# The six-layer stage: own tables of places for each engine and batch, hand-over by single banks, norm steps on VectorE and ScalarE

## The chip, the cores and the metric

The kernel runs on one core of one Trainium2 chip. Its time is the device time of one execution in microseconds; the kernel before takes 3076.7 us (median of 3 runs, 3075.34 to 3079.2). Another execution was recorded by the hardware profiler, and the rows below are from that one.

The engines are PE (TensorE), DVE (VectorE), ACT (ScalarE), POOL (GpSimd) and SP (SyncE, which only issues transfers here). Each executes its own list of instructions in order. They meet only at semaphores: an instruction with an unmet wait holds back everything behind it on its engine. All matrix products land in PSUM, which has 8 banks of 2 KB in each of 128 partitions; one bank holds a 128x512 product in f32.

## The reference

The program is four residual blocks on x of shape (2, 512, 128): a cross-attention transformer block (stage A), an attention block with 31 routed experts (stage B), six layers of self-attention, cross-attention and feed-forward (stage C), and a block with 64 experts (stage D). The change is in stage C only. What it computes, per batch of two:

```
for i in range(6):                                   # D=128, 16 heads of 8, DFF=512, context 77
    xn = adaln(x, noise, n1_w[i], n1_b[i])           # layernorm, then scale and shift
    q, k, v = split(xn @ qkv_w[i].T)
    x = x + attn(rope(q), rope(k), v, src_mask) @ so_w[i].T       # 512 x 512 scores, 16 heads
    xn = adaln(x, noise, n2_w[i], n2_b[i])
    x = x + attn(rope(xn @ cq_w[i].T), rope(ctx @ ck_w[i].T),
                 ctx @ cv_w[i].T, ctx_mask) @ co_w[i].T           # 512 x 77 scores
    xn = adaln(x, noise, n3_w[i], n3_b[i])
    x = x + gelu(xn @ f1_w[i].T + f1_b[i]) @ f2_w[i].T + f2_b[i]
```

## The kernel before

Stage C (`stage_c`, line 1372) works through 12 units: unit n is layer n // 2 of batch n % 2. A unit starts from the result of unit n - 2, so that two chains of six units run beside each other.

A unit is: layernorm statistics on DVE (`stats`), the reciprocal root, the normalised tiles, four transposes on PE (`turn_norm`) and the scale and shift on ACT (`copy_norm`, into `hT`). Then the products for q, k (each with a rotated twin) and v. Since the scores are computed from bf16 operands without loss, q and k are cut into three bf16 parts on DVE, ACT and POOL, and 12 transfers on SP stack these parts in `qs` and `ks` (`stack`).

Self-attention takes 32 tiles twice. In the first pass `scores` multiplies and DVE takes the row maxima (`row_max`, L2042); each tile is two products, one for each half of the array's rows (`hp` 0 is partitions 0 to 63, `hp` 1 is 64 to 127), in PSUM banks 0 and 1. The maxima of a quarter are split in two bf16 parts, turned on PE (`turn_max`), copied by ACT and stacked as two more rows of `qs` by SP (`stack_max`). In the second pass `scores_T` multiplies again, transposed, with the maximum already subtracted (banks 2 and 3), ACT takes the exponential (`exps`, L1899), and PE weighs the values (`weigh`, L1525, bank 4). The sums go by ACT (`copy_sums`), PE (`turn_back`) and DVE (`normalise`) into `cn`.

Cross-attention has the same two passes in smaller form (`cross_max` with L2097 on DVE, `cross_T` with L1943 on ACT, `weigh_x`, `turn_back_x`). Everything but the two large passes shares a ring of three banks (5, 6, 7) through `fill`, `arrived` and `drained`: a bank's next use waits for the last one's reader.

In the kernel before, the norm is shared by two engines. DVE takes the statistics and a bit-trick seed of the reciprocal root (`seed_steps`); POOL then does three Newton steps of four small operations (`newton_steps`, L102 to L105) and writes the four normalised tiles (`apply`, L1831).

What sets the order of the work: each engine's list is written out by the same double loop over windows of 48 places, and the same tables serve all engines and both batches. `S_AT`, `ST_AT` and `W_AT` say at which place the tiles of the two passes stand, the `C_...` names where the other steps stand. Unit n's first pass begins in window n; its second pass runs into the next one; its cross-attention and feed-forward (`rest`) are in window n + 1, beside the self-attention of unit n + 1; the start of unit n + 2 (`begin`) comes at places 32 to 41 of that window. At one place an engine takes the steps in a fixed sequence: score products, `rest`, `begin`, `weigh` and the turns. `scores(n, i)` and `scores_T(n, j)` emit both halves in a row.

## Time and profile before

| | us |
|---|---|
| median of 3 runs | 3076.7 |
| the profiled execution | 3073.5 |
| its span | 3071.7 |
| stage C in it, from its first statistics of a unit (1082.67) to its last addition of a unit (begins 2818.84) | 1736.2 |
| its steady part, 1118 to 2694 | 1576, of which PE busy 1271.7 |
| two units (2027.96 to 2301.03) | 273.07 |

Most of the rows are of three kinds. A window row gives the busy time of every engine in a stretch and the granted clock of TensorE, where 1.00 is 2.4 GHz and 0.50 is 1.2 GHz. A timeline row is one instruction or a run of equal ones: its start, its length, and in square brackets how long the engine had been idle before it and what ended that. A row of groups gives the number of instructions, their busy time in all and the mean of one. PE's busy time counts each product up to its modelled end, so two products that run side by side, or one behind the other in the pipeline, overlap in it.

### The profile page before, as it was taken

Reading aid. Unit: us, or ns where it says so; the run is one execution under the profiler, and the core shown is the slowest. Engines: PE = TensorE matmul, PEld = TensorE weight load, DVE = VectorE, ACT = ScalarE, POOL = GpSimd, SP = SyncE. Lnnn points to the kernel's source line nnn. Section 1 sums busy time; section 2 is a strip of 40 time slices with the busy share of each in tenths; the row PEclk is TensorE's granted clock in tenths of the full one; section 3 lists DMA queues with packets and bytes.
Section 4 is the critical chain, followed back from the end, with each engine's and each line's share of the span. In section 5 each row is a group of like instructions: output and inputs, shape, how many; then the busy total and the mean of one; then the engine's idle time right before and its main releaser. Section 6 shows DMA issues by size and latency. Waiting matters only on the chain. (4 is left out here: it accounts for less than half of the span.)

```text
span 3071.7 us, 31900 instructions
## 1 busy us (share of the span) xinstructions
PE 2470.8 (80%) x11288; PEld 978.6 (32%) x11288; DVE 1591.5 (52%) x3349; ACT 1113.9 (36%) x1840; POOL 344.5 (11%) x719
## 2 busy tenths in 40 slices
...
GB/s 123 1 1 1 0 1 1 97 1 1 1 1 1 10 72 21 1 21 1 36 1 21 36 1 21 1 36 1 21 19 18 21 1 21 1 1 85 1 0 7
DMA packets 38095, 54.33 MB, mean 18 GB/s; under 512 B 5137, under 2 KB 34610, under 8 KB 36402
## 3 DMA queue, kind: packets, MB, share of 16 engines
...
## 5 line engine op out<-in xcount | busy, mean ns | idle before, releaser
L2042 DVE TENSOR_REDUCE C_nm<-ps 128x1 f32<-128x512 f32 x768 | 491.3, 684 | 384.3 <-PE ps L1489 375.2
L1899 ACT ACTIVATE C_prob<-ps 128x512 f32<-128x512 f32 x768 | 415.3, 593 | 324.0 <-PE ps L1510 300.3
L1489 PE MATMUL ps<-C_ks,C_qs 62*128 62x512 bf16 x768 | 253.2, 496 | 102.3 <-DVE C_nm L2042 82.8
L1510 PE MATMUL ps<-C_qs,C_ks 64*128 64x512 bf16 x768 | 214.8, 446 | 51.3 <-ACT C_prob L1899 41.5
L1525 PE MATMUL ps<-C_prob,C_va 128*32 128x512 f32 x1536 | 233.7, 688 | 0.4
L1489 PEld LDWEIGHTS ps<-C_ks,C_qs 62*128 62x128 bf16 x768 | 50.9, 97 | 365.8 <-DVE C_nm L2042 233.9
L102 POOL TENSOR_TENSOR lnt<-rs 128x4 f32<-128x4 f32 x108 | 21.4, 198 | 1278.6 <-DVEq L2036 1272.9
L1606 PE MATMUL ps<-C_kc,C_qx 32*128 32x308 f32 x384 | 122.1, 724 | 29.3 <-DVE C_nmx L2097 13.0
L1943 ACT ACTIVATE C_u<-ps,C_biasx 77x512 f32<-77x512 f32 x192 | 120.7, 677 | 68.2 <-PE ps L1633 61.2
L1629 PE MATMUL ps<-C_qx,C_kc 32*77 32x512 f32 x384 | 128.7, 749 | 20.4 <-ACT C_u L1943 11.6
L714 DVE TENSOR_REDUCE A_nm<-ps 128x2 f32<-128x1024 f32 x64 | 77.5, 1212 | 113.8 <-PE ps L497 113.6
L1564 PE MATMUL ps<-ident,xn 128*128 128x128 f32 x144 | 35.6, 394 | 121.1 <-POOL xn L1831 121.1
L2064 DVE RECIPROCAL C_rden<-ps 128x16 f32<-128x16 f32 x96 | 24.6, 256 | 198.3 <-PE ps L1533 134.8
L1921 ACT ACTIVATE C_hT<-ps,aff 128x512 f32<-128x512 f32 x36 | 28.0, 777 | 267.4 <-PE ps L1564 267.4
L1831 POOL TENSOR_SCALAR xn<-y,mv,rs 128x128 f32<-128x128 f32 x144 | 112.4, 793 | 3.9
L2097 DVE TENSOR_REDUCE C_nmx<-ps 128x4 f32<-128x308 f32 x192 | 82.8, 473 | 51.0 <-PE ps L1610 50.5
L1571 PE MATMUL ps<-C_hT,C_w 128*128 128x512 f32 x144 | 101.8, 847 | 5.5 <-ACT C_hT L1921 5.5
L647 ACT ACTIVATE A_p<-ps 128x1024 f32<-128x1024 f32 x64 | 65.6, 1025 | 112.1 <-PE ps L525 112.1
L647 ACT ACTIVATE B_p<-ps 128x1024 f32<-128x1024 f32 (+1 forms) x64 | 45.0, 703 | 146.6 <-PE ps L529 146.6
L1510 PEld LDWEIGHTS ps<-C_qs,C_ks 64*128 64x128 bf16 x768 | 48.5, 98 | 150.5 <-ACT C_prob L1899 104.0
L455 PE MATMUL ps<-hT,B_w 128*128 128x512 f32 x128 | 75.6, 674 | 23.4 <-DVE B_rot L709 12.2
L1303 DVE SCALAR_TENSOR_TENSOR y<-ps,B_gates,y 128x128 f32<-128x128 f32 x256 | 71.9, 344 | 42.0 <-PE ps L1257 42.0
...
## 6 DMA issues: line engine op xcount, KB each, us to landing
...
B_w<-in_B_ew SPq DMA_DIRECT2D x8, 514.0 KB, 10.5
...
```

Of the source, the lines that this page charges most:

```text
L647: act.activation(prob[:, n % 2, kt, :, q0:S], ps[:, ST_BANK:ST_BANK + 2, q0:S], ACT.Exp, scale=SCALE)\
L1489: pe.matmul(ps[:, S_BANK + hp, :], lhsT=qs[side(hp, MAX_ROW), b, 2 * q + pq, t * P:(t + 1) * P], rhs=ks[side(hp, MAX_ROW), b, 2 * q + pq, ...
L1510: pe.matmul(ps[:, ST_BANK + hp, :], lhsT=ks[side(hp, HALF), b, 2 * q + pq, kt * P:(kt + 1) * P], rhs=qs[side(hp, HALF), b, 2 * q + pq, :], ...
L1525: last = pe.matmul(ps[ct * VW:(ct + 1) * VW, PV_BANK, :], lhsT=va[:, b, kt, q * QUAD + ct, :], rhs=prob[:, kt % 2, ct // 2, ct % 2, :], st ...
L1571: pe.matmul(ps[:, bank, :], lhsT=weight(n, col), rhs=hT[:], start=True, stop=True)\
L1606: pe.matmul(ps[:, banks[gh], 0:4 * CTX], lhsT=qx[rows, t * P:(t + 1) * P], rhs=cross.k[rows, c, :, :], start=True, stop=False)
L1629: pe.matmul(ps[0:CTX, banks[gh], :], lhsT=cross.k[rows, c, j, :], rhs=qx[rows, :], start=True, stop=False)
L1831: ins = pool.tensor_scalar(m.xn[:, k, :], m.y[:, k, :], m.mv[:, t, 0:1], m.rs[:, t:t + 1], ALU.subtract, ALU.mult)
L1899: act.activation(prob[:, kt % 2, pq, hp, :], ps[:, ST_BANK + hp, :], ACT.Exp, scale=SCALE)\
L1943: act.activation(probx[:, q % 2, jj, gh, :], ps[0:CTX, bank, :], ACT.Exp, bias=cross.bias[:, b:b + 1], scale=SCALE).then_inc(emptied[bank], 1)
L2042: dve.tensor_reduce(nm[:, q % 2, t, pq, hp:hp + 1], ps[:, S_BANK + hp, :], AX.X, ALU.max, negate=True).then_inc(max_done, 1)
L2097: dve.tensor_reduce(nmx[:, t, 8 * gp + 4 * gh:8 * gp + 4 * gh + 4], ps[:, bank, 0:4 * CTX].rearrange("p (j k) -> p j k", k=CTX), AX.X, ALU ...
```

## The change

Four things change, all in stage C.

1. Each engine gets its own table for even units (batch 0) and odd units (batch 1): `TENSOR`, `VECTOR`, `SCALAR`, `GPSIMD`, `SYNC`. A table gives each step a place; `WINDOW` is 1128, unit n's places are counted from 1128 n, and an engine's list is all its steps sorted by that sum (`timeline`). Places of a unit reach from 208 to 2456 (even) and from 0 to 2242 (odd).
2. The two halves of a score tile, the twins of q, k and the cross query, and the four products and four gelus of the feed-forward become steps with places of their own. A wait for the previous reader then covers one bank rather than a pair. The semaphore of the parts is divided in one for q and one for k, and k comes before q.
3. The norm: all of the reciprocal root is now on DVE (`rstd_steps`, 12 small operations, and one for minus mean times root), and the product and shift that make the normalised tiles are four `Identity` activations on ACT (`apply`). POOL keeps one addition and two subtractions for k, the copy of `vx` and the bias.
4. The rotated cross query uses `hT` of the norm's buffer (`m.hT`) instead of a part of `rot`; `copy_norm` waits for the last reader of `hT`. The zeroing of `qs` and `ks` on POOL no longer stands behind a norm.

```diff
-WINDOW = 48
-S_AT = [1, 2, 2, 3, 4, 5, 5, 6, 7, 8, 9, 11, 12, 13, 14, 15,
+WINDOW = 1128
+TENSOR = (
+    {"S": [453, 464, 469, 485, 501, 518, 534, 551, 567, 584, 598, 615, 620, 636, 641, 658, 670, 675, 694, 702,
...
+def timeline(tables):
+    return sorted({(n * WINDOW + s, n, s) for n in range(UNITS) for slots in tables[n % B].values() for s in slots})
...
-        rotx = rot[:, 0, :, :]
+        rotx = m.hT
...
-                def scores(n, i):
+                def scores(n, i, hp):
...
-                    for hp in range(2):
-                        if n or i:
-                            pe.wait_ge(max_done, 2 * (n * TILES + i) + hp - 1)
-                        pe.matmul(ps[:, S_BANK + hp, :],
...
+                    if n or i:
+                        pe.wait_ge(max_done, 2 * (n * TILES + i) + hp - 1)
+                    pe.matmul(ps[:, S_BANK + hp, :],
...
-                cp = Chain(pool, order_p)
-
-                def apply(n, count):
-                    pool.wait_ge(seeded, count)
-                    newton_steps(cp, pool, m, TB)
-                    for t in range(TB):
-                        k = n % B * TB + t
-                        ins = pool.tensor_scalar(m.xn[:, k, :], m.y[:, k, :], m.mv[:, t, 0:1], m.rs[:, t:t + 1],
-                                                 ALU.subtract, ALU.mult)
...
+                def apply(n, count):
+                    act.wait_ge(seeded, count)
+                    for t in range(TB):
+                        k = n % B * TB + t
+                        ins = act.activation(m.xn[:, k, :], m.y[:, k, :], ACT.Identity, bias=m.lnu[:, t:t + 1],
+                                             scale=m.rs[:, t:t + 1])
+                    ins.then_inc(xn_ready, 1)
...
-                    seed_steps(c_, dve, m, TB, False)
-                    dve.sem_inc(seeded, 1)
+                    rstd_steps(c_, dve, m, TB, False)
+                    dve.scalar_tensor_tensor(m.lnu[:, 0:TB], m.mv[:, 0:TB, 0], -1.0, m.rs[:, 0:TB], ALU.mult, ALU.mult)\
+                        .then_inc(seeded, 1)
...
-                    for i in ((0, 1, 2), (3,))[k]:
-                        bank = fill(("ff", c, i))
-                        pe.matmul(ps[:, bank, :], lhsT=weight(c, LF1 + i * P), rhs=hT[:], start=True, stop=True)\
-                            .then_inc(filled[bank], 1)
+                    bank = fill(("ff", c, i))
+                    pe.matmul(ps[:, bank, :], lhsT=weight(c, LF1 + i * P), rhs=hT[:], start=True, stop=True)\
+                        .then_inc(filled[bank], 1)
...
-                for n in range(UNITS + 1):
-                    for s in range(WINDOW):
-                        if n:
-                            score(n - 1, s + WINDOW)
...
+                for _, n, s in timeline(TENSOR):
+                    step(n, s)
```

Some places of the tables, odd units: on PE the products of the first pass stand at 235 to 1047 and those of the second at 456 to 1350, the first cross score step at 1569, the feed-forward's last step at 2206. On DVE the maxima stand 8 places apart where they are densest, the three norms' statistics at 0, 1453 and 2046. Even units: first pass 453 to 1328, second 755 to 1526, first cross score step 1749, last step 2419 on PE and 2456 on DVE.

Three pieces of the lists follow, each before and after. PE, at the first pass over the cross scores of a batch, beside the other batch's self-attention. `C_kc,C_qx` and `C_krowc,C_onesc` are one half of a cross score step (keys and mask row), `C_ks,C_qs` a product of the first pass, `C_qs,C_ks` one of the second. Before:

```order
L1606 MATMUL ps<-C_kc,C_qx 128x308 x2
L1610 MATMUL ps<-C_krowc,C_onesc 128x308 x2
L1489 MATMUL ps<-C_ks,C_qs 128x512 x2
L1510 MATMUL ps<-C_qs,C_ks 128x512 x2
L1618 MATMUL ps<-identb,C_nmpx 128x128 x4
L1629 MATMUL ps<-C_qx,C_kc 77x512 x2
```

and after:

```order
L1675 MATMUL ps<-C_ks,C_qs 128x512
L1791 MATMUL ps<-C_kc,C_qx 128x308 x2
L1795 MATMUL ps<-C_krowc,C_onesc 128x308 x2
L1675 MATMUL ps<-C_ks,C_qs 128x512 x2
L1803 MATMUL ps<-identb,C_nmpx 128x128 x4
L1675 MATMUL ps<-C_ks,C_qs 128x512
L1814 MATMUL ps<-C_qx,C_kc 77x512 x2
L1818 MATMUL ps<-C_nmTx,C_selx 77x512 x2
```

Where a round held one cross step, a pair of the first pass and a pair of the second, it now holds one cross step and one or two single products of the first pass.

DVE, from the addition of an attention's result (`y<-y,ps`) over the statistics to the seed of the norm. Before:

```order
L2042 TENSOR_REDUCE C_nm<-ps 128x1 x8
L2072 TENSOR_TENSOR y<-y,ps 128x512
L2028 BN_STATS st<-y 128x6 x4
L2031 BN_AGGR mv<-st 128x2 x4
L93 TENSOR_SCALAR lnv<-mv 128x4
L94 TENSOR_SCALAR lnt<-lnv 128x4
L95 TENSOR_SCALAR rs<-lnt 128x4
L2042 TENSOR_REDUCE C_nm<-ps 128x1 x8
```

and after:

```order
L2205 TENSOR_TENSOR y<-y,ps 128x512
L2175 TENSOR_REDUCE C_nm<-ps 128x1
L2161 BN_STATS st<-y 128x6 x4
L2164 BN_AGGR mv<-st 128x2 x4
L2175 TENSOR_REDUCE C_nm<-ps 128x1
L93 TENSOR_SCALAR lnv<-mv 128x4
L94 TENSOR_SCALAR lnt<-lnv 128x4
L95 TENSOR_SCALAR rs<-lnt 128x4
L79 TENSOR_TENSOR lnt<-rs 128x4
L80 SCALAR_TENSOR_TENSOR lnu<-lnt,lnv 128x4
L81 SCALAR_TENSOR_TENSOR rs<-lnu,rs 128x4
```

The last three rows come three times, and one `lnu<-mv,rs` (L2169) behind them; single maxima stand between the parts of the norm.

ACT, around the third norm and the feed-forward of an odd unit (`C_prob` is an exponential of the second pass, `C_cT` the copy of the turned context, `xn` the normalised tiles, `C_hT` the scale and shift, `C_u` with x4 the gelus). Before:

```order
L1899 ACTIVATE C_prob<-ps 128x512 x6
L1915 ACTIVATE C_cT<-ps 128x512
L1910 ACTIVATE C_nmT<-ps 8x512
L1899 ACTIVATE C_prob<-ps 128x512 x2
L1921 ACTIVATE C_hT<-ps,aff 128x512
L1899 ACTIVATE C_prob<-ps 128x512 x2
L1956 ACT_TABLE_LOAD
L1956 ACTIVATE C_u<-ps,C_w 128x512 x4
```

and after:

```order
L2034 ACTIVATE C_prob<-ps 128x512 x7
L2039 ACTIVATE C_cw<-ps 128x512
L2034 ACTIVATE C_prob<-ps 128x512
L2065 ACTIVATE xn<-y,lnu,rs 128x128 x4
L2034 ACTIVATE C_prob<-ps 128x512 x2
L2058 ACTIVATE C_hT<-ps,aff 128x512
L2034 ACTIVATE C_prob<-ps 128x512 x2
L2138 ACT_TABLE_LOAD
L2138 ACTIVATE C_u<-ps,C_w 128x512 x4
```

The four tiles of the norm have come in, two exponentials ahead of the scale and shift; the gelus stay together between two table loads.

## Rows read from the trace of the kernel before

**Rows 1.** The page: busy time of each engine, share of the span, instructions.

```profile
PE 2470.8 (80%) x11288; PEld 978.6 (32%) x11288; DVE 1591.5 (52%) x3349; ACT 1113.9 (36%) x1840; POOL 344.5 (11%) x719
```

**Rows 2.** Windows: stretch, its length, busy time of each engine, PEclk granted clock.

```profile
1118.00:2694.00 1576.00, 1271.70 (x6083) 442.56 (x6081) 791.24 (x1790) 727.51 (x1284) 242.83 (x585) 0.77 0.05 15
2028.00:2301.10 273.10, 220.62 (x1066) 77.34 (x1066) 134.23 (x305) 127.08 (x224) 43.80 (x106) 0.78 0.06 16
2048.50:2055.30 6.80, 2.40 (x4) 0.40 (x4) 4.67 (x13) 0.00 (x0) 4.74 (x16) 0.50 0.00 0
2069.00:2089.00 20.00, 17.60 (x70) 5.29 (x70) 12.23 (x26) 6.20 (x11) 0.00 (x0) 0.50 0.00 1
2089.40:2123.60 34.20, 30.70 (x208) 10.22 (x204) 16.71 (x36) 25.14 (x45) 0.00 (x0) 1.00 0.01 1
```

**Rows 3.** Waits of PE from 1118 to 2694: total us, times, longest.

```profile
PE ps L1489 <- DVE C_nm L2042: 82.8, 113, 3.0
PE ps L1564 <- POOL xn L1831: 78.1, 33, 3.2
PE ps L1510 <- ACT C_prob L1899: 38.1, 70, 0.8
```

**Rows 4.** Timeline: a unit's stage C start, end, and same step two units apart.

```profile
1082.67 0.87 DVE L2028 BATCH_NORM_STATS2 st<-y 128x6 f32<-128x128 f32 x4
1117.70 0.61 PE L1489 MATMUL ps<-C_ks,C_qs 62*128 62x512 bf16 x2 [16.14 <-DMA C_ks<-C_parts]
2027.96 0.58 SPq L1761 DMA_DIRECT2D C_qs<-C_parts  x1
2301.03 0.58 SPq L1761 DMA_DIRECT2D C_qs<-C_parts  x1
2818.84 0.69 DVE L2122 TENSOR_TENSOR y<-y,ps 128x512 f32<-128x512 f32 x1 [18.65 <-PE ps L1660]
```

**Rows 5.** Timeline: the second norm of the last unit, from DVE over POOL to PE.

```profile
2721.63 0.17 DVE L93 TENSOR_SCALAR lnv<-mv 128x4 f32<-128x4 f32 x1
2721.84 0.17 DVE L94 TENSOR_SCALAR lnt<-lnv 128x4 int32<-128x4 int32 x1
2722.35 0.20 POOL L102 TENSOR_TENSOR lnt<-rs 128x4 f32<-128x4 f32 x1 [43.12 <-DVEq L2036]
2725.73 3.12 POOL L1831 TENSOR_SCALAR xn<-y,mv,rs 128x128 f32<-128x128 f32 x4
2728.91 1.11 PE L1564 MATMUL ps<-ident,xn 128*128 128x128 f32 x4 [9.35 <-POOL xn L1831]
```

**Rows 6.** Groups of instructions, 2028 to 2301: count, then busy us, mean ns.

```profile
L2042 DVE TENSOR_REDUCE C_nm<-ps 128x1 f32<-128x512 f32 x128 | 82.0, 684 | 65.8 <-PE ps L1489 64.3
L1899 ACT ACTIVATE C_prob<-ps 128x512 f32<-128x512 f32 x128 | 69.2, 593 | 53.3 <-PE ps L1510 49.3 <-PE ps L1525 3.3
L1970 ACT ACTIVATE C_va<-ps,C_valid 128x128 f32<-128x128 f32 x8 | 2.3, 368 | 1.9 <-PE ps L1577 1.9
L1921 ACT ACTIVATE C_hT<-ps,aff 128x512 f32<-128x512 f32 x6 | 4.7, 777 | 39.2 <-PE ps L1564 39.2
L1899 ACT ACT_TABLE_LOAD x2 | 2.6, 1283 | 0.0
```

**Rows 7.** Timeline of PE: a cross score round, then score pairs at the other clock.

```profile
2211.16 1.40 PE L1606 MATMUL ps<-C_kc,C_qx 32*128 32x308 f32 x4
2212.74 0.61 PE L1489 MATMUL ps<-C_ks,C_qs 62*128 62x512 bf16 x2
2213.14 0.64 PE L1510 MATMUL ps<-C_qs,C_ks 64*128 64x512 bf16 x2
2213.71 1.40 PE L1606 MATMUL ps<-C_kc,C_qx 32*128 32x308 f32 x4
2245.15 0.39 PE L1489 MATMUL ps<-C_ks,C_qs 62*128 62x512 bf16 x2
2245.38 0.38 PE L1510 MATMUL ps<-C_qs,C_ks 64*128 64x512 bf16 x2
```

818 lines of the change are left out of this document (456 added, 362 removed), and 28 rows, old and new, of tables (SCALAR, TENSOR, VECTOR).

## The prediction, on record before the changed kernel ran

> **What bounds the kernel now.** I read the page first. PE is the busiest engine, DVE has half the span and nothing else is near [rows 1]. Then the windows: the change is confined to stage C, so its steady part counts. There PE is busy 1271.7 of 1576 us, DVE 791 and ACT 728, at a mean granted clock of 0.77 [rows 2]. No engine is full. Two units take 273.07 us [rows 4], so a unit takes 136.5 us, of which PE is busy 110.3, DVE 67.1 and ACT 63.5 (halves of the second row) [rows 2]. PE's idle time is three waits: for the row maxima 82.8 us, for POOL's normalised tiles 78.1, for exponentials 38.1 [rows 3].
>
> The reader is to see two things. First, the order leaves holes: after a norm's seed PE has 2.40 us of work in 6.8, since the tables stop the other batch too while POOL works. Second, the holes and the clock go together. The clock is 0.50 in that hole, and still 0.50 in the 20 us behind it, though PE is busy 17.6 of them; it is 1.00 in the 34 us after, with PE busy 30.7 [rows 2]. A unit is thus a chain of hand-overs through three engines, about half of it on a PE at 1.2 GHz.
>
> **Norm steps.** From POOL's first Newton operation (2722.35) to PE's transposes (2728.91) are 6.56 us [rows 5]. After it, nine operations and one more on DVE at 0.21 us each (2721.63 to 2721.84) [rows 5] are 2.1 us. The activation on a 128x128 f32 tile with scale and bias per partition is not in the trace. Below, a quarter of the 128x512 one of the same kind, 0.19 us; above, POOL's own 0.78 (3.12 for four) [rows 5, 6]. The nearest row is the 128x128 copy with a scale, 0.37 us with its end and less back to back [rows 6]; I take 0.3, so 1.2 for four, between 0.8 and 3.1. The chain becomes 3.3 us and 3.2 are saved (1.3 to 3.6). A unit has three norms, 9.6 us, and its own chain extends over two windows (unit n + 2 needs its result), so each window gains 4.8 us.
>
> What is queued behind: DVE's root now holds back maxima for 2.7 us (13 x 0.21), and with two banks PE's first pass stops for that time; DVE also waits for ACT's tiles before its next statistics, because the means and roots have one buffer. ACT's four tiles hold back exponentials for 1.2 us, and behind these the second pass and `weigh`. Loads per unit: DVE 67.1 + 30 x 0.21 = 73.4, ACT 63.5 + 3.6 = 67.1 (up to 72.8). Both are far below any period discussed here, so this costs order, not capacity. POOL leaves the path.
>
> **Single banks.** Two products on different halves of the rows run side by side: the pair of the first pass starts 0.23 us before the pair of the second (2245.15, 2245.38) and 0.40 at the lower clock (2212.74, 2213.14) [rows 7], about one product's time. Split into single steps, a product shares only if its neighbour uses the other half. Counted in the new table over two units, of 256 products 82 ride with a neighbour and 174 do not; before, 128 did not. That is 23 more per unit, at 0.23 to 0.40 us: PE pays 5.3 to 9.2 us. In return each bank is freed alone. The waits that this can shorten are the 82.8 and 38.1 us of [rows 3], 10.5 us per unit over 11.5 units: it pays back at most about what it costs. I book it at nothing, between 9 us lost and 5 gained.
>
> The Trainium skill, TensorEngine Tiling (Array Packing), Key Properties, says that different tiles of the array work in parallel; by that rule alone every lone half-array product is a loss. The trace agrees with the 0.23 us for two.
>
> **Own tables.** Places only sort; how long one lasts must come from rows. Maxima stand 8 places apart and last 0.684 us [rows 6]: 0.086 us a place. The 13 small operations of a root have 24 places: 0.11. From the last gelu of an odd unit to the next exponential are 20 places for a gelu (about one exponential, 0.593) and a table load of 1.283 [rows 6]: 0.094. So a window of 1128 lasts between 96 and 128 us, if every engine keeps to its places; at 0.1 us a place, 112.8. The binding places are the mixed chains of the norm and the hand-overs, so I take 0.1, not the smallest.
>
> The table's own cross-check is PE. Its 110.3 us at a clock of 0.78 are at most 86.0 us at 1.00; with 23 x 0.23 more, 91.3. Nothing idle, that fits into 107 us at a clock of 0.85 and into 117 at 0.78. So 112.8 needs a clock above 0.81. (The busy time overstates PE, as the pairs show: 0.39 us long, 0.23 apart [rows 7], so this is a strict test.) Does the clock rise? The holes behind the seeds shrink, as the other batch's maxima, exponentials and products now stand in them. But for even units the table still has one: from v (place 331) to the second norm's transposes of the odd unit (386) PE has only v. Behind it come that unit's cross score rounds at 1.2 GHz. A round is now 2.55 us (2211.16 to 2213.71) [rows 7]; without the second-pass pair (0.57) and one shared product it is about 1.95, where the table has 16.5 places, 1.65. Eight rounds and the rest of a cold stretch run some 3 to 4 us late. I take a mean clock of 0.85 and PE idle for 8%: 107.4 / 0.92 = 116.7. Against the table's 112.8 plus half of the 6 to 7 us by which the cold stretches of two units run late, 116. I forecast 116 us for a window.
>
> **The start** of the stage: from the first statistics to the first product are 35.0 us (1082.67 to 1117.70) [rows 4], in the table 245 places, 24.5. The zeroing of `qs` and `ks` no longer waits behind a norm on POOL, and 12 small transfers on SP with it, so I keep the table's; if not, it costs 10 us.
>
> **The sum.** From the first statistics (place 208) to the last addition (11 x 1128 + 2242 = 14650) are 14442 places, 12.80 windows. At 116 us: 1485 us, where the trace has 1736.2 (2818.84 - 1082.67) [rows 4]. The profiled execution's 3073.5 becomes 2822.5; the median of the runs is 3.2 above it, so 2826. Of the 251 us, the norms are 4.8 x 12.8 = 61, the start 10, the tables and the clock 180. The likeliest case's own range is a window of 109 to 123 us, 2736 to 2915.
>
> **Rivals.**
> (A) The table is kept or beaten. The rows allow 0.086 us where maxima or exponentials pace it, and with no cold stretch PE needs 91. For it: ACT and DVE are under 75 us. Against it: the hole at place 331. A window of 106 gives 1357 and 2698. 12%.
> (B) The clock stays as it is or falls. PE now waits bank by bank, and where it waited after a hole it stayed at 0.50 for 20 us while busy [rows 2]. At a mean of 0.76 and PE idle for 8% a window is 91.3 / 0.76 / 0.92 = 130: 1664 and 3005. Against it: in the hot stretch PE also waited now and then, and stayed at 1.00 [rows 2]. 10%. The Trainium skill, TensorE: Matmul & The Clock Gate, A second HAM failure mode: psum-queue depth-cycling, describes this: short idle times between matmul groups as PSUM banks cycle make the clock go back and forth. No row here shows it inside a hot stretch.
> (C) The tables bring nothing beyond the norms: what they gain in holes the single banks lose. 61 us: 3016. For it, PE's 117 us at today's clock; against it, POOL's 78 us of PE idle was filled by nobody. 4%.
> (D) Slower. The lone products make PE the bound at the low clock: the cold stretches grow together until PE is always busy. With 91.3 us of full-clock work and nothing idle, the window exceeds today's 136.5 once the mean clock is below 0.67. At 0.65 it is 140.5: 1799 and 3139. For it: a 20 us stretch with PE 88% busy at 0.50. Against it: it needs 70% of the time at 1.2 GHz, today it is about 45%. 5%.
> (E) No change: 3%, the windows between these, with 135.6 us each.
>
> **How the numbers follow.** My forecast 66%, A 12, B 10, C 4, E 3, D 5. The range from 2720 to 2985 leaves out some 7% of A, 3 of B, C, D and E: about 2 in 10. About 0.2% of the time (6 us) is what a measurement tells from no change. Faster by more: 66 + 12 + 10 + 4 = 92%; same 3%; slower 5%.
>
> **What would show it.** In the new profile two units should be 232 us apart (225.6 by the table, 273 today); from a norm's root to PE's transposes about 1.5 us, from the end of its seed 3.3; the four activations about 1.2; PE's wait for normalised tiles under 30 us in all; PE's busy time per unit near 100 us and the granted clock in the stage near 0.85; DVE at 73 and ACT at 67 us per unit. A low clock behind place 331 of even units, and nowhere else for long, would confirm the hole. Stage D and stages A and B should not move. I am wrong in mechanism if the clock stays at 0.77 while the window falls below 117, if the products of the first pass wait for maxima for more than now, or if the time falls by less than 100 us.

## The result, and the profile after

The changed kernel takes 3014.3 us (median of four runs, 2970.5 to 3031.1); the kernel before, run beside it on the same chip, 3078.0. It is faster, by 64 us or 2.1%; 251 us were forecast, and 3014 lies above the range of 2720 to 2985. The ratio on record is 0.971, 95% interval 0.967 to 0.975: ratios here leave out executions more than 1.5% above the fastest of their kernel (two of these four), so for a kernel that scatters they lean to the fast side. A second set of six runs (e1 below, none left out) gives 3004.2, ratio 0.978 (0.974 to 0.981). The profiled execution shown here is the slowest of the ten: 3031.1 us, span 3029.3. In these two sets the runs of the kernel before lie within 0.4%, those of the changed one are 2% apart.

The steady part of the stage, and then its four full layers one by one (a layer is two units, from the even unit's stacking to the next one's). Columns as in [rows 2]:

```profile
1118.00:2694.00 1576.00, 1384.69 (x6192) 447.44 (x6192) 861.37 (x2147) 799.77 (x1447) 56.88 (x56) 0.76 0.06 15
1346.11:1613.90 267.79, 235.61 (x1067) 75.77 (x1066) 146.09 (x365) 137.06 (x248) 10.29 (x10) 0.78 0.07 17
1613.90:1897.43 283.53, 252.17 (x1067) 78.86 (x1066) 146.34 (x365) 136.92 (x248) 10.28 (x10) 0.72 0.06 16
1897.43:2187.28 289.85, 259.37 (x1067) 81.28 (x1066) 146.37 (x365) 137.56 (x248) 10.30 (x10) 0.69 0.06 16
2187.28:2442.76 255.48, 225.05 (x1065) 75.70 (x1064) 145.58 (x363) 136.29 (x248) 10.29 (x10) 0.81 0.07 18
```

Before, a layer took 273.1 us each time. Now the same list of instructions takes 255 to 290 us, and the clock goes the other way: 0.81 in the shortest, 0.69 in the longest. The waits of PE in 1118 to 2694, beside [rows 3]:

```profile
PE ps L1749 <- ACT xn L2065: 44.9, 22, 6.3
PE ps L1675 <- DVE C_nm L2175: 37.2, 70, 2.1
PE ps L1695 <- ACT C_prob L2034: 32.5, 69, 0.8
PE ps L1675 <- DMA C_qs<-C_parts: 22.4, 5, 9.4
```

The waits for maxima went from 82.8 to 37.2 us and those for normalised tiles from 78.1 to 44.9. With the four layers added up (a layer's us, PE's busy us, the clock of the stretch, and busy times clock, PE's work in us at 2.4 GHz):

| | layer | PE busy | clock | work |
|---|---|---|---|---|
| before | 273.1 | 220.5 | 0.77 | 170 |
| changed, the profile above | 274.2 | 243.0 | 0.75 | 182 |
| changed, e1 | 266.1 | 234.2 | 0.78 | 183 |

PE's idle time in a layer fell from 52.6 to 31.1 us, and all of it came back as busy time: 12 us of added work, which I put down to products that no longer share the array, and the lower clock. In the profile above the four layers are no shorter than before. Its whole gain is behind them: from the last even unit's stacking to the last addition are 333.3 us (2442.76 to 2776.08), before 383.6 (2435.22 to 2818.84, [rows 4]). In e1 the four layers also gain, 28 us in all. That is where executions of this kernel differ from each other.

What decides where the clock falls is not visible in the rows, and one place shows it. These are 103 us from the same place of the list in two neighbouring layers, 290.75 us apart (each a stretch of 20 us and the 83 us behind it):

```profile
2048.00:2068.00 20.00, 17.49 (x95) 6.09 (x91) 16.95 (x47) 12.66 (x24) 0.29 (x1) 1.00 0.01 2
2068.00:2151.00 83.00, 81.94 (x281) 19.78 (x280) 30.20 (x63) 31.77 (x55) 0.00 (x0) 0.50 0.00 1
2338.75:2358.75 20.00, 17.49 (x95) 6.08 (x91) 16.95 (x47) 12.55 (x24) 0.29 (x1) 1.00 0.01 2
2358.75:2441.75 83.00, 76.27 (x426) 29.06 (x426) 40.91 (x115) 52.45 (x93) 2.22 (x2) 0.94 0.00 1
```

The first and third row have the same products and the same busy time of PE, 17.49 us. Then the clock falls in one layer and stays. On the timeline of PE, the rows at which they part:

```profile
2067.73 0.39 PE L1675 MATMUL ps<-C_ks,C_qs 62*128 62x512 bf16 x1
2068.05 1.92 PE L1710 MATMUL ps<-C_prob,C_va 128*32 128x512 f32 x8
```

```profile
2358.48 0.39 PE L1675 MATMUL ps<-C_ks,C_qs 62*128 62x512 bf16 x1
2358.80 1.06 PE L1710 MATMUL ps<-C_prob,C_va 128*32 128x512 f32 x8
```

In the 83 us after it PE is busy for 81.94, at 1.2 GHz, and gets through 281 products where the other layer does 426. What it does there, by groups of its products (the form behind the names, as 64*128, is rows times columns of the array that a product uses):

```profile
L1695 PE MATMUL ps<-C_qs,C_ks 64*128 64x512 bf16 x30 | 16.3, 611 | 0.0
L1814 PE MATMUL ps<-C_qx,C_kc 32*77 32x512 f32 x32 | 15.9, 1091 | 0.4 <-ACT C_u L2127 0.4
L1710 PE MATMUL ps<-C_prob,C_va 128*32 128x512 f32 x64 | 15.5, 1059 | 0.7 <-ACT C_prob L2034 0.7
L1675 PE MATMUL ps<-C_ks,C_qs 62*128 62x512 bf16 x29 | 14.8, 608 | 0.0
L1791 PE MATMUL ps<-C_kc,C_qx 32*128 32x308 f32 x28 | 9.8, 796 | 0.0
```

None of the five, 72 of the 97 us, uses the whole array (busy times of products that overlap add up to more than the 83 us). A PE that has hardly a pause can stay at 1.2 GHz for 80 us. The other layer runs products of the same kinds at 0.94, so the kind alone does not decide it. The prediction had not reckoned with that. The Trainium skill (TensorE: Matmul & The Clock Gate, What's actually happening) says that activity releases the throttle; by PE's busy time this row does not agree, 81.94 of 83 us at 0.50.

The norm of the last unit, which answers to [rows 5], from the first operation of the root to the transposes:

```profile
2684.72 0.17 DVE L93 TENSOR_SCALAR lnv<-mv 128x4 f32<-128x4 f32 x1
2687.09 0.16 DVE L2169 SCALAR_TENSOR_TENSOR lnu<-mv,rs 128x4 f32<-128x4 f32 x1
2687.29 1.65 ACT L2065 ACTIVATE xn<-y,lnu,rs 128x128 f32<-128x128 f32 x4 [5.86 <-DVE lnu L2169]
2688.99 1.11 PE L1749 MATMUL ps<-ident,xn 128*128 128x128 f32 x4 [6.35 <-ACT xn L2065]
```

4.27 us, where [rows 5] had 7.28: 3.0 saved, 3.2 forecast. The four activations take 1.65, not 1.2.

### The profile page after: what moved, and what is told of

The parts are those of the page before. It is cut to its first block and busy times, and to the rows that moved or that the text cites. A ratio compares the mean times of both kernels' runs of the same rounds, so it can differ in the third digit from the quotient of the medians.

```text
span 3029.3 us, 32357 instructions
## 1 busy us (share of the span) xinstructions
PE 2559.8 (85%) x11288; PEld 973.1 (32%) x11288; DVE 1677.7 (55%) x3709; ACT 1174.1 (39%) x1984; POOL 143.0 (5%) x143
## 5 line engine op out<-in xcount | busy, mean ns | idle before, releaser
L2175 DVE TENSOR_REDUCE C_nm<-ps 128x1 f32<-128x512 f32 x768 | 508.0, 685 | 334.1 <-PE ps L1675 329.1
L2034 ACT ACTIVATE C_prob<-ps 128x512 f32<-128x512 f32 x768 | 429.6, 594 | 248.5 <-PE ps L1695 242.3
L1675 PE MATMUL ps<-C_ks,C_qs 62*128 62x512 bf16 x768 | 312.8, 478 | 61.0 <-DVE C_nm L2175 37.2
L1695 PE MATMUL ps<-C_qs,C_ks 64*128 64x512 bf16 x768 | 287.4, 442 | 35.5 <-ACT C_prob L2034 32.5
L1814 PE MATMUL ps<-C_qx,C_kc 32*77 32x512 f32 x384 | 171.1, 981 | 10.9 <-ACT C_u L2127 9.5
L1675 PEld LDWEIGHTS ps<-C_ks,C_qs 62*128 62x128 bf16 x768 | 63.9, 98 | 305.8 <-DVE C_nm L2175 163.9
L2197 DVE RECIPROCAL C_rden<-ps 128x16 f32<-128x16 f32 x96 | 24.5, 255 | 154.2 <-PE ps L1725 135.3
L1755 PE MATMUL ps<-C_hT,C_w 128*128 128x512 f32 x144 | 88.9, 743 | 7.7 <-ACT C_hT L2058 7.5
L2529 ACT ACTIVATE D_g<-ps 128x512 f32<-128x512 f32 (+1 forms) x66 | 39.4, 597 | 143.9 <-PE ps L2491 143.9
L2546 DVE TENSOR_TENSOR D_t<-D_g,ps 128x512 f32<-128x512 f32 x64 | 44.0, 688 | 89.3 <-PE ps L2495 89.3
L2065 ACT ACTIVATE xn<-y,lnu,rs 128x128 f32<-128x128 f32 x144 | 59.1, 483 | 61.6 <-DVE lnu L2169 60.9
## 6 DMA issues: line engine op xcount, KB each, us to landing
D_w<-in_D_ew SPq DMA_DIRECT2D x8, 768.0 KB, 11.3
```

The lines of the kernel that those rows point to most:

```text
L1675: pe.matmul(ps[:, S_BANK + hp, :], lhsT=qs[side(hp, MAX_ROW), b, 2 * q + pq, t * P:(t + 1) * P], rhs=ks[side(hp, MAX_ROW), b, 2 * q + pq, ...
L1695: pe.matmul(ps[:, ST_BANK + hp, :], lhsT=ks[side(hp, HALF), b, 2 * q + pq, kt * P:(kt + 1) * P], rhs=qs[side(hp, HALF), b, 2 * q + pq, :], ...
L1755: pe.matmul(ps[:, bank, :], lhsT=weight(n, col), rhs=hT[:], start=True, stop=True)\
L1814: pe.matmul(ps[0:CTX, banks[gh], :], lhsT=cross.k[rows, c, j, :], rhs=qx[rows, :], start=True, stop=False)
L2034: act.activation(prob[:, kt % 2, pq, hp, :], ps[:, ST_BANK + hp, :], ACT.Exp, scale=SCALE)\
L2175: dve.tensor_reduce(nm[:, q % 2, t, pq, hp:hp + 1], ps[:, S_BANK + hp, :], AX.X, ALU.max, negate=True).then_inc(max_done, 1)
```

## The experiments

Each kernel ran beside the kernel before, and ratios are to that. Differences between two variants of the changed kernel are told by the medians of all their executions; the two sets of the changed kernel differ by 10 us (3014.3 and 3004.2), and the kernel before moves from 3074 to 3080 from one set to the next, so less than 10 us is not told apart.

**e1. The changed kernel again**, unedited.

> The changed kernel as it is, to see how far its executions differ from each other. Theory C (clock): its list is long stretches at 1.2 GHz that begin or fail to begin by chance, so that executions differ by 20 to 60 us, where those of the kernel before agree within 7, and a higher mean clock goes with a shorter time, about 2.5 us for each 0.001 of the mean granted clock over the span. Rival O (order): the time is set by hand-overs in a fixed list; then executions agree within 10 us and the clock is the same in all.

3004.2 us (2986.4 to 3030.2), ratio 0.978 (0.974 to 0.981). Time and mean clock of its six executions go together: 2986.4 at 0.839, 2991.1 at 0.837, 3003.6 at 0.828, 3004.7 at 0.831, 3016.5 at 0.824, 3030.2 at 0.819. That is 2.2 us for each thousandth of the clock (43.8 us over 0.020): the scatter goes with the clock, as theory C said.

**e2. The kernel before with the norm's new split only**: whole root on DVE, tiles on ACT, old tables.

```diff
-                    seed_steps(c_, dve, m, TB, False)
-                    dve.sem_inc(seeded, 1)
+                    rstd_steps(c_, dve, m, TB, False)
+                    dve.scalar_tensor_tensor(m.lnu[:, 0:TB], m.mv[:, 0:TB, 0], -1.0, m.rs[:, 0:TB], ALU.mult, ALU.mult)
```
(and `apply` moved from POOL's list to the same places of ACT's)

> The kernel before with the norm steps of the change alone: whole root on VectorE, tiles on ScalarE, old tables and pairs of halves. Theory N (the prediction's term): 3.2 us less in each of three norms of a unit whose chain extends over two windows, so 4.8 us a window: 60 us less than before, near 3018, which would be nearly all of the measured gain. Rival P (the other engines pay): VectorE's 2.7 us of small operations and ScalarE's tiles, which stand in the fixed order ahead of maxima and exponentials, give most of it back: less than 25 us gained, above 3053. Rival C (clock): PE idles for less, the clock rises above 0.821, gain more than 60.

3171.9 us, ratio 1.031 (1.029 to 1.033): 94 us slower. PE no longer waits for tiles in the steady part, and still loses. Its longest waits in 1118 to 2694, beside [rows 3]:

```profile
PE ps L1489 <- DVE C_nm L2040: 117.0, 113, 4.7
PE ps L1510 <- ACT C_prob L1879: 71.9, 80, 3.6
```

The 78 us for POOL's tiles turned into 34 more for maxima and 34 more for exponentials: as I read it, a wait that one idle engine had carried is now carried by the two engines that feed PE, and each holds back its own list (rival P, by far). On top of it the clock fell, as the rows under e4 show.

**e12. The half of e2**: root on DVE, tiles still on POOL.

> The kernel before with only the root moved: VectorE does the whole reciprocal root (12 small operations), GpSimd still writes the four normalised tiles (3.1 us). The kernel before took 3077, with the tiles on ScalarE too it took 3171.9. Theory O (it is the tiles on ScalarE that hurt, since they stand in its fixed list and hold back exponentials): this kernel is at or below 3077, down to 3050 as 2 us per norm are saved. Theory K (each wait that closes before TensorE's list leaves it longer at 1.2 GHz: TensorE was busy 96 us longer and idle as long as before when both moved): already the shorter wait costs, 3090 to 3150 us. Rival V (the root on VectorE holds back maxima): PE's wait for maxima rises from 83 us towards 121, with the granted clock unchanged.

3055.5 us, ratio 0.994 (0.992 to 0.996): 19 us faster than before. Its two longest waits in the same stretch:

```profile
PE ps L1489 <- DVE C_nm L2043: 121.2, 112, 4.8
PE ps L1510 <- ACT C_prob L1898: 41.5, 75, 0.9
```

The wait for maxima is as long as in e2, that for exponentials is as before. So the root on DVE is worth its price even in the old order, and what costs e2 its 116 us against this kernel is that the tiles stand in ACT's list: theory O. A part of the 116 us is the clock, which is 0.77 here over e4's stretch below and 0.72 in e2. Rival V was right about the maxima, and wrong that they decide.

**e3. The changed kernel with the old split of the norm**: Newton steps and tiles back on POOL, at ACT's places of the new tables.

> The changed kernel with the Newton steps and the tiles back on GpSimd (the tables and single banks stay). Theory N: each window of about 135 us becomes 4 to 5 us longer, 50 to 60 us more than the changed kernel, near 3070. Rival P: the norm steps bring nothing in this order, since VectorE and ScalarE are relieved by as much: within 15 us of the changed kernel. Rival C: the hole in which PE waits 5.7 us for the second norm grows to about 9 us, and stretches at 1.2 GHz become longer too: 80 us more or above.

3164.1 us, ratio 1.021 (1.017 to 1.026): 160 us more than e1. PE waits 140.5 us for POOL's tiles (31 times, up to 10.5), where it waits 45 for ACT's. That is rival C's side. The new split of the norm is worth 160 us in the new tables and costs 94 in the old. The new tables were written for the time that the new split takes; the old split doesn't fit in it.

**e4. Both halves of a score tile issued together** on PE, at the later one's place.

```diff
+for at in TENSOR:
+    for key in ("S", "ST"):
+        for k in range(0, 2 * TILES, 2):
+            at[key][k] = at[key][k + 1]
```

> The changed kernel, where on PE both halves of each tile of the two passes stand at the place of the later one, so that they run side by side again; all other engines keep their lists. Theory L (lone products keep PE busy at 1.2 GHz, and there it is the bound): PE saves 23 products of 0.23 to 0.40 us per unit, and in stretches at 1.2 GHz with PE always busy they count in full: 60 to 110 us less than the changed kernel. Rival S (single hand-over is what pays): maxima and exponentials wait for the pair again, 30 us more or above. Within 20 us either way: gain and loss cancel, as the prediction booked them.

3067.8 us, ratio 0.998 (0.995 to 1.000): 64 us more than e1, rival S. In these tables the hand-over by single banks is worth most of the gain; the other engines' lists are still those written for singles, so this is not what pairs would cost in tables of their own. The wait for maxima grows to 51.5 us, that for exponentials to 46.8. The clock, in the same stretch for the kernel before, the changed one in the slow execution shown above and in e1, then e2 and e4 (in this order):

```profile
1118.00:2550.00 1432.00, 1155.29 (x5492) 399.45 (x5494) 720.48 (x1629) 658.78 (x1164) 220.94 (x532) 0.77 0.05 15
```

```profile
1118.00:2550.00 1432.00, 1263.69 (x5510) 405.23 (x5510) 777.58 (x1942) 709.71 (x1282) 51.45 (x50) 0.74 0.06 15
```

```profile
1118.00:2550.00 1432.00, 1245.11 (x5753) 405.88 (x5753) 817.36 (x2031) 744.39 (x1352) 56.32 (x55) 0.80 0.07 17
```

```profile
1118.00:2550.00 1432.00, 1166.90 (x5149) 390.00 (x5148) 712.81 (x1815) 666.12 (x1212) 54.51 (x50) 0.72 0.05 15
```

```profile
1118.00:2550.00 1432.00, 1173.82 (x5537) 387.84 (x5538) 773.12 (x1948) 702.37 (x1290) 51.46 (x50) 0.77 0.06 15
```

The changed kernel has 0.74 in its slowest execution and 0.80 in one of its faster ones, so a variant's clock is to be held against both. Pairs don't give a better one: 0.77 here, and over the whole of its executions 0.804 to 0.825 where e1 has 0.819 to 0.839. And PE is idle for 258 of 1432 us, in e1 for 187. e2 does 5149 products where the kernel before does 5492, with PE as long busy: that part of its loss is the clock.

**e5. The hole of odd units filled.** Ahead of the transposes of an odd unit's second norm, five f32 products of constants, whose bank the transposes overwrite.

```diff
+                    bank = fill(key)
+                    for _ in range(5 if key[0] == "hT2" and b == 1 else 0):
+                        pe.matmul(ps[:, bank, :], lhsT=m.ident[:], rhs=cos[:], start=True, stop=True)
                     pe.wait_ge(xn_ready, count)
-                    bank = fill(key)
```

> The changed kernel with five products of no use (128x128 by 128x512, f32) on PE ahead of the second norm's transposes of odd units, written to the bank that these transposes overwrite. There PE now waits 5.7 us in each of six layers, is at 2.4 GHz for the first 3 us of it and at 1.2 GHz for the 60 to 70 us behind it. The products last 4.3 us at 2.4 GHz, so they fit in the wait. Theory C (the hole's price is the clock behind it): PE does more work and the kernel becomes faster: 15 to 30 us less per layer, 90 to 180 us less than the changed kernel, with the mean clock above 0.86. Rival M (the clock follows what kind of products PE has there, cross scores on 32 rows and lone halves, not the hole): the clock falls all the same within some us, time within 20 us of the changed kernel. Rival B (PE was not the bound there): the clock rises but the time stays.

3024.5 us (2956.8 to 3065.4), by the medians 0.984 of the kernel before: no gain, rival M's side. Its executions scatter more than e1's, and two of the six (2956.8 and 2972.9) are faster than any of e1; the profile is of the fastest. The clock did what the filler was for, and it did not last. Windows of e5, from the transposes (2115.53) to the first cross score round, and behind it:

```profile
2115.60:2121.50 5.90, 3.34 (x14) 1.48 (x14) 3.44 (x5) 1.69 (x3) 0.22 (x1) 1.00 0.50 133
2122.00:2174.00 52.00, 49.36 (x158) 13.86 (x160) 25.70 (x51) 13.95 (x23) 0.00 (x0) 0.51 0.00 1
```

The wait of 5.66 us shrank to 0.90 and the clock was 1.00 behind it; in the cross score rounds it fell all the same, with PE busy 49 of 52 us. The hole was where I said, and filling it did not keep the clock up.

**e6. The next layer's weights loaded later.** In an odd unit the load of 1090 KB stood ahead of the parts of q on SP's queue; here it stands behind all of them.

```diff
                     if s in at["PART_Q"]:
-                        if n % B and n > B and layer(n) + 1 < LAYERS:
-                            drained(sp, ("f2", n - B))
-                            load(layer(n) + 1)
...
                         stack(n, 0, 2)
+                        if n % B and n > B and layer(n) + 1 < LAYERS:
+                            drained(sp, ("f2", n - B))
+                            load(layer(n) + 1)
```

> The changed kernel with the load of the next layer's weights (1090 KB) moved on SyncE from ahead of the odd unit's q parts to behind all its stacking transfers. Now its first-pass product at place 235 waits 2.7 to 3.6 us for these parts in four layers, with exponentials' products queued behind it, and the clock is at 1.2 GHz for 15 to 25 us after. Theory Q (the load is in the way of the parts): the wait shrinks to under 1 us, and with it 4 x 3 = 12 us by itself and up to 4 x 10 us more by the clock: 12 to 50 us less than the changed kernel. Rival: the transfers are late by their own chain (sum, parts, remainders), the wait stays above 2 us and the time within 10 us.

2969.9 us, ratio 0.962 (0.958 to 0.966): 34 us less than e1. In the changed kernel SP's queue reads

```profile
2302.82 3.16 SPq L1925 DMA_DIRECT2D C_ks<-C_parts  x5
2306.03 0.59 SPq L1912 DMA_DIRECT2D C_w<-in_C_w  x1
2306.66 1.86 SPq L1925 DMA_DIRECT2D C_qs<-C_parts  x3
```

and PE waits for the parts behind it, 2.7 us at 2316 and 3.4 at 2026.8 (22.4 in all). With the load behind them the row is

```profile
PE ps L1675 <- DMA C_qs<-C_parts: 9.9, 1, 9.9
```

One wait is left, that of the stage's start. 12.5 us of waits went and 34 of time. I put the rest down to the clock behind such a wait (in the changed kernel 0.59 in the 25 us from 2315), though that part isn't shown by itself.

**e7. e5 and e6 together.**

> Both edits: five filling products in the odd units' norm wait and the late weight load. Theory C: the two gains add up, 100 to 200 us less than the changed kernel and the lowest time of all. Rival M: no more than the late load alone gives.

2961.8 us (2925.3 to 2986.8), ratio 0.959 (0.954 to 0.963). With the late load or without, the filler's worth isn't told apart from nothing.

**e8. The filler in the kernel before** (three products).

> The kernel before with three filling products ahead of the second norm's transposes of units 1 to 11, where PE waits about 3.2 us for GpSimd's tiles (2.6 us of products at 2.4 GHz). Theory C: a part of the 1.2 GHz stretch of 35 us behind that norm goes and the kernel becomes 30 to 100 us faster. Rival M: the clock is 0.50 behind it all the same, and since PE is often at 1.2 GHz already when the wait begins, the products last 5 us and cost 10 to 20 us in all.

3088.9 us, ratio 1.005 (1.003 to 1.007): 14 us slower, as rival M had it.

**e9. Full-row bf16 products among the cross scores**, two at the head of each round of odd units, on top of e7.

```diff
+                    for _ in range(2 if c % B else 0):
+                        pe.matmul(ps[:, banks[0], :], lhsT=m.identb[:],
+                                  rhs=cross.sel[:].rearrange("p h k -> p (h k)")[:, 0:S], start=True, stop=True)
```

> The changed kernel with the late weight load and the five extra products in the wait of odd units (2961.8 us, ratio 0.9586), plus two bf16 products of all 128 rows (identity, 512 columns) at the head of each of the 8 first-pass cross score rounds of odd units, written to a bank that the round's own product overwrites. 0.22 us each at 2.4 GHz, so 3.5 us a layer, 21 us over six layers if nothing else changes. Theory M (the clock falls in the cross score rounds because the products there use 32 or 64 of the 128 rows, so that full-row work mixed in holds it): the clock stays at 1.00 through the rounds, the mean of the stage rises by 0.03 or more and the time is under 2940 us. Rival I (it is not the rows of the products, or two are too few): the clock falls in the rounds as before, and the products cost their own time at 1.2 GHz as well: 2980 to 3000 us.

2973.9 us, ratio 0.966 (0.963 to 0.970): 12 us more than e7, between the two expectations and nearer to rival I's. The clock still falls in the rounds; over e4's stretch it is 0.82, where e7 has 0.81. Two such products a round may be too few.

**e10. GpSimd's zeroing held back** until the stage's first root is done (`pool.wait_ge(seeded, 1)` ahead of the zeroing of `qs` and `ks`).

> The changed kernel with one wait added on GpSimd: the zeroing of qs and ks and the making of the selection matrix start only when the stage's first reciprocal root is done. Theory G (VectorE's small operations are slowed while GpSimd writes SBUF: the 128x8 operation of 10.9 us and its alternately 0.17 and 1.27 us neighbours are this): the root of the stage's first norms takes 0.17 to 0.2 us an operation, the first statistics end some 12 us earlier than 1096, and the time falls by 8 to 14 us against the changed kernel (3004 to 3014), since the transfers that stack the constant rows come later by a part of that. Rival W (they are slowed by something else, a semaphore or the weight load of 1090 KB): the 10.9 us operation stays and the time does not fall by 5 us.

3019.9 us, ratio 0.977 (0.972 to 0.982): no gain that can be measured, though the slow operations went where theory G said. DVE ahead of the stage in the changed kernel, the first operations of the root of the norm that leads into it:

```profile
1071.54 10.91 DVE L93 TENSOR_SCALAR lnv<-mv 128x8 f32<-128x8 f32 x1
1082.48 1.05 DVE L94 TENSOR_SCALAR lnt<-lnv 128x8 int32<-128x8 int32 x1
1083.57 0.17 DVE L95 TENSOR_SCALAR rs<-lnt 128x8 int32<-128x8 int32 x1
1083.77 1.27 DVE L79 TENSOR_TENSOR lnt<-rs 128x8 f32<-128x8 f32 x1
```

POOL beside it, back to back from 1069.14:

```profile
1075.46 3.50 POOL L2014 MEMSET C_qs<- 128x4096 f32 x1
1078.91 3.50 POOL L2014 MEMSET C_ks<- 128x4096 f32 x1
1082.37 1.14 POOL L2015 MEMSET C_selx<- 128x1232 bf16 x1
1083.65 12.12 POOL L2018 TENSOR_SCALAR_AFFINE_SELECT C_selx<-C_selx 128x1232 bf16<-128x1232 bf16 x8
```

and DVE in e10:

```profile
1072.75 4.00 DVE L93 TENSOR_SCALAR lnv<-mv 128x8 f32<-128x8 f32 x1
1076.78 0.17 DVE L94 TENSOR_SCALAR lnt<-lnv 128x8 int32<-128x8 int32 x1
1085.06 8.11 DVE L2315 TENSOR_SCALAR C_biasx<-C_mkc 77x2 f32<-77x2 uint8 x1
1085.13 8.56 DVE L2316 TENSOR_SCALAR C_krow<-C_mrow 1x1024 bf16<-1x1024 uint8 x1
```

The root of the stage's first unit ends at 1085.05 instead of 1100.2, and then the small operations behind it stand for 8 us, as the zeroing has moved beside them. They make the constant rows that SP stacks, and PE's first product waits for SP: it starts at 1117.59, against 1120.49. The stall was moved, not removed.

**e11. e7 and e10 together.**

> The late weight load, the five extra products in the wait of odd units (together 2961.8 us, ratio 0.9586) and the wait on GpSimd of the kernel before in this call. If the three act on different places they add: 2948 to 2954 us, ratio about 0.955. If the start does not matter, 2962.

2945.1 us (2923.1 to 2972.9), ratio 0.956 (0.953 to 0.959). It is the fastest kernel here that computes the reference. Its interval and that of e7 overlap.

**e13. All score products over all 128 rows.** Half of the rows of a score product belong to the other head; here they are summed in, so the kernel computes something else. Banks, columns, waits and order are those of the changed kernel. The exponential's scale is multiplied by 1e-6, so that the products that weigh the values get numbers near 1.

```diff
-                              lhsT=qs[side(hp, MAX_ROW), b, 2 * q + pq, t * P:(t + 1) * P],
-                              rhs=ks[side(hp, MAX_ROW), b, 2 * q + pq, :], start=True, stop=True)\
+                              lhsT=qs[:, b, 2 * q + pq, t * P:(t + 1) * P],
+                              rhs=ks[:, b, 2 * q + pq, :], start=True, stop=True)\
```
(the same in the second pass)

> The changed kernel, with every score product of both passes over all 128 rows of the array instead of 62 or 64 of them. It computes the sum of two heads' scores for each, so the result is another; the exponential's scale is multiplied by 1e-6 to keep it finite. Columns, banks, waits and order are the same. Two neighbours can no longer run side by side: of 256 products in two units 82 did, so 41 a unit at 0.23 us at 2.4 GHz, 9 us a unit more for TensorE. Theory R (the clock falls because these products use half of the rows, and recovers late for the same reason): the clock of the steady part rises from 0.75 to 0.95 or more, the window falls to 105 to 113 us, and the time to 2700 to 2850 us. Rival I (the rows don't matter for the clock): it stays near 0.75, TensorE has 100 us of full-clock work a window, and the time is 3050 to 3150 us.

2881.1 us (2875.5 to 2892.8), ratio 0.937 (0.935 to 0.939). 123 us less than e1, with more for PE to do, and the scatter is down to 0.6%. The direction is theory R's; time and clock (0.88 in the table's stretch below) both stay short of its ranges.

**e14. The cross scores over all rows too**, and e13's edit, on top of e11; the scale of both exponentials is multiplied by 1e-6.

> The same with the cross scores over all 128 rows too (instead of 32), on top of the kernel with the late weight load, the five extra products and the wait on GpSimd (2945.1 us). Its result is another as well, and the scale of both exponentials is multiplied by 1e-6. Theory R: no stretch at 1.2 GHz of over 20 us is left in the steady part, the clock is 0.97 or more, 2650 to 2780 us. Rival I: 3000 to 3130 us at a clock of the steady part of 0.75 to 0.80.

2900.7 us (2895.5 to 2906.4), ratio 0.942 (0.940 to 0.944). The clock is what theory R said, the time is not: see the table. Ten microseconds in the cross scores of one unit, in e13 (cross scores still on 32 rows) and in e14:

```profile
1370.00:1380.00 10.00, 9.83 (x32) 2.59 (x33) 3.74 (x7) 3.10 (x6) 0.00 (x0) 0.50 0.00 1
```

```profile
1370.00:1380.00 10.00, 9.66 (x40) 3.08 (x41) 4.70 (x11) 4.18 (x8) 0.00 (x0) 1.00 0.00 0
```

In e13 the clock is 0.50 from 1340 to 1380, and the largest part of PE's work there is cross score products on 32 rows, beside full-row products of the first pass.

**e16. The control of e13: both halves from the same 64 rows**, so that nothing runs side by side and no more rows are used than before.

```diff
-        side = lambda hp, rows: slice(HALF * hp, HALF * hp + rows)
+        side = lambda hp, rows: slice(0, rows)
```

> The changed kernel, where both halves of a score tile are computed from the rows 0 to 63: 62 or 64 rows as before, but always the same ones, so that two neighbours can't run side by side, as in the full-row kernel (2881.1 us, clock of the steady part 0.88). The second head of each pair is the first again, so its result is another. Theory R (it is the number of rows in a product that counts for the clock): the clock stays at 0.72 to 0.78, TensorE has 9 us a unit more to do and the time is 3040 to 3150 us. Rival T (it is the longer occupation of TensorE, as nothing overlaps): the clock goes to 0.85 to 0.90 and the time to 2870 to 2900 us as with full rows.

3154.3 us (3150.1 to 3195.1), ratio 1.027 (1.023 to 1.031). e13 and e16 issue the same number of products with the same columns, at the same places, and in both none overlaps; the rows differ, and the data with them, and the exponential's scale, which e16 leaves as it is; 273 us lie between the two. The stretch of e4's rows in e13, e14 and e16:

```profile
1118.00:2550.00 1432.00, 1240.74 (x6093) 454.99 (x6204) 862.17 (x2154) 794.48 (x1450) 58.12 (x57) 0.88 0.07 17
```

```profile
1118.00:2550.00 1432.00, 1278.52 (x6125) 497.44 (x6237) 851.86 (x2125) 790.17 (x1442) 56.70 (x55) 0.97 0.06 17
```

```profile
1118.00:2550.00 1432.00, 1318.56 (x5205) 411.44 (x5205) 744.62 (x1839) 676.80 (x1213) 50.13 (x49) 0.71 0.06 16
```

0.74 and 0.80 in the changed kernel, 0.88 with full rows in the self-attention's scores, 0.71 in the control; 0.84 in e11, and 0.97 with full rows in all scores on top of it. Over whole executions the clock says the same without overlap: 0.819 to 0.839 in e1, 0.870 to 0.878 in e13, 0.779 to 0.789 in e16; and 0.838 to 0.860 in e11, 0.927 to 0.932 in e14. Rival T falls, and theory R holds in direction. One rival stands beside it: the small scale makes the exponentials nearly equal numbers in e13 and e14 (and in e15), and no run changes the scale alone. The ten microseconds under e14 speak against it: there, only 1.7 of PE's 9.7 us are products that read an exponential, and the clock is up where the cross scores have all rows.

**e15. Faster readers**: maximum and exponential over half of a tile's columns, the exponential's scale multiplied by 1e-3.

> The changed kernel, where the maximum of a score tile is taken over 256 of its 512 columns, and from the second unit on the exponential too (its scale is multiplied by 1e-3 to keep it finite): half of each row is left out of both. The maximum then takes about 0.35 us instead of 0.68 and the exponential 0.35 instead of 0.59, so that TensorE waits less than now for either (68 of 175 us of its idle time). Theory W (these short waits make the clock fall): the clock of the steady part rises above 0.90, 2750 to 2880 us. Theory R (the kind of product makes it fall): the clock stays at 0.70 to 0.80, the waits for maxima and exponentials go, and the time falls by at most the 68 us, 2940 to 2990 us, with stretches of 40 us and more at 1.2 GHz as before.

2917.4 us (2879.7 to 2934.5), ratio 0.942 (0.938 to 0.946), clock of the stretch 0.83 (the changed kernel has 0.74 and 0.80). 87 us less than e1, so between the two expectations: PE's waits for maxima and exponentials fell only from 72 to 48 us in the steady part, and the mean clock over whole executions is 0.840 to 0.859, above e1's, though stretches of 68 us and more at 1.2 GHz remain. The short waits seem to have a share in the clock, where theory R gave them none; the scale was changed here too, so that share isn't shown by itself.

**e17 and e18. Full-row products beside the half-row ones**, ahead of each product of the first pass (e17: all units; e18: even units), on top of e11.

```diff
+                    if True:
+                        pe.matmul(ps[:, S_BANK + hp, 0:S], lhsT=m.identb[:], rhs=qs[:, b, 2 * q + pq, 0:S],
+                                  start=True, stop=True)
```

> The kernel with the late weight load, the five extra products and the wait on GpSimd (2945.1 us), with one bf16 product over all 128 rows and 512 columns ahead of each product of the first pass, into the same bank, where the real product overwrites it. 64 a unit at 0.22 us, 13.8 us a unit more for TensorE at 2.4 GHz. Theory R: with a third of the score products now full-row the stretches at 1.2 GHz shrink, the clock of the steady part rises to 0.90 or more and pays for the added work: 2840 to 2930 us. Rival L (added work costs more than the clock gives): 2960 to 3100 us.

> The same, with the added products only in even units, whose first pass fills the part of a layer in which the stretches at 1.2 GHz lie: 6.9 us a unit more. Theory R: 2860 to 2930 us, the part of a layer from the even to the odd unit's stacking falls from about 112 us to 100. Rival L: 2950 to 3020 us.

e17: 3154.1 us, ratio 1.024 (1.022 to 1.027). e18: 3122.6 us, ratio 1.013 (1.010 to 1.016). Both miss theory R's ranges by far, and lie 54 and 103 us above rival L's as well. e17's clock is 0.85 in the stretch, where e11 has 0.84, and a layer takes 289.4 us with PE busy for 271.9. Full-row products beside half-row ones hardly raised the clock, and as PE was the bound already, their time came on top. What is gained must come from the products that are there.

The layers of all of them (means of four full layers, columns as in the first table):

| | layer | PE busy | clock | work |
|---|---|---|---|---|
| e11, best that computes the reference | 250.8 | 225.7 | 0.84 | 190 |
| e13, full rows | 244.1 | 214.0 | 0.87 | 186 |
| e14, full rows everywhere | 245.4 | 220.7 | 0.98 | 216 |
| e16, the control | 295.4 | 275.3 | 0.69 | 190 |
| e15, half readers | 249.1 | 218.6 | 0.82 | 179 |

(e13 and e14 lack a few records of products, 4183 where the changed kernel has 4257, so their busy time is a little low.) In e14 PE runs nearly always at full speed, and a layer is no shorter than in e13: 30 us more work a layer eat what the clock gives, for the most part, I think, because four cross score products no longer share the array. PE is idle for 25 us of 245 there. If the changed kernel's 182 us of work ran at 2.4 GHz with that idle time, a layer would take 207, a unit 103.5 (an estimate from these rows): by that estimate the tables themselves leave room for the forecast's 116. No kernel here had both.

## Why the prediction was wrong

**The step that failed is the clock.** I took a mean clock of 0.85 and PE idle for 8%, hence 116 us for a window. PE's work at 2.4 GHz was forecast as 91.3 us a unit and is 91 (182 for two). PE's idle share is 11.3% (31.1 of 274.2 us). The clock is 0.75. With the forecast clock and the measured idle share, 91.3 / 0.85 / 0.887 is 121; with 0.75 it is 137, and 137.1 is measured. So of the 21 us by which a window is late, 5 are idle time and 16 are the clock. That is the slowest execution, and its four full layers only. In e1, with a clock of 0.78 and 12.0% idle, the same sum gives 133.0, and 133.1 is measured: 17 us late, 6 by idle time and 11 by the clock. Over 12.8 windows the clock's part is 205 us by the one and 140 by the other; the forecast is 188 and 178 us below the medians. Part of the rest is the end of the stage, which ran better than its middle.

**Why I chose 0.85.** I reasoned that the clock is low behind holes, so that fewer holes make it rise. The one hole that I named is there: until 2193.53 PE waits 5.66 us for the tiles, and it is then at 0.50, in this profile for 65 us. The row of it:

```profile
2193.53 1.11 PE L1749 MATMUL ps<-ident,xn 128*128 128x128 f32 x4 [5.66 <-ACT xn L2065]
```

I allowed 3 to 4 us for its aftermath. And when it was filled (e5) the clock fell a few us later. What the runs put in its place is the kind of the products: with 62 or 64 of the 128 rows in the scores and 32 in the cross scores, the clock of the stretch is 0.74 or 0.80, and 0.84 in e11; with all rows in use in both it is 0.97, and e16 excludes that it comes from products that no longer overlap. The rows are not all of it: e15 has 0.83 with the rows as they were. In [rows 2] there was a sign that I did not weigh: 20 us with PE busy 17.6 of them and the clock at 0.50 throughout, in which 58 of 70 products use half of the rows or fewer. I put it down to the 6.8 us hole ahead of it. It would not have settled the matter, as the 34 us behind it at 1.00 hold such products too.

**Rival B is what happened.** It took 91.3 us of work at a clock of 0.76 with 8% idle, 130 us a window and 3005 us; the medians are 3014 and 3004. I gave it 10%. The nearness of the time is partly luck: its mechanism, PE that waits bank by bank, is at most a part, as e15 takes a third of such waits away and gives 0.83, with the exponential's scale changed besides.

**The norm.** The chain got shorter by 3.0 us as forecast (3.2). The step that a window gains 4.8 us from it, 61 in all, fails: e2 shows that the new split costs 94 us where the order doesn't provide for it, e3 that it is worth 160 where it does. It can't be priced apart from the tables. I had named what is queued behind (maxima for 2.7 us, exponentials for 1.2) and called it order, not capacity; e2 and e12 price that order at 116 us for the tiles in ACT's list alone, clock included. The wait for tiles fell to 44.9 us, not under 30.

**Single banks.** Booked at nothing, between 9 lost and 5 gained a unit. PE's work grew by 6 us a unit (170 to 182 for two), inside the 5.3 to 9.2. But the other side was worth more: e4 loses 64 us without it, over 12 units 5.3 each net, just beyond the upper end, and in tables that were written for singles. The added work agrees with what the Trainium skill says (TensorEngine Tiling (Array Packing), Key Properties), that different tiles work in parallel: a lone one is a loss, here of 6 us a unit.

**A place at 0.1 us.** Right where the clock is high. From an odd unit's stacking to the next even unit's are 1331 places; in e1's fastest full layer they take 135.9 us (2255.25 to 2391.19) at a clock of 0.94, 0.102 a place. From even to odd are 925 places, which take 115.5 us at a clock of 0.70, 0.125 a place.

**The start** was forecast 10 us shorter. From DVE's first statistics of the stage to the first product it is 24.1 us (1096.38 to 1120.49), as the tables have it (24.5, before 35.0). But the statistics themselves come 13.7 us later than in [rows 4], since POOL's zeroing now runs beside the norm ahead of them (e10 holds it back, and they come at 1081.18). I had written that it no longer waits behind a norm on POOL, and not asked what it would now stand beside. The first product is 2.8 us later than before.

**The other rivals.** A (2698) needed the table kept with no cold stretch; only e14 has almost none, and it has 17 us a unit more to do. C gives 3016, the measured time, for a reason that is false: the tables did bring something, the norm alone brings a loss. D wanted PE always busy at a clock below 0.67; the worst layer (0.69, 290 us, PE busy 259) comes near it, and e16, another kernel, nearer (0.69, 295 us, PE busy 275). Of what I said would show the mechanism wrong, one came true: the time fell by less than 100 us.
